# A transformer layer's first stage in another order: input and one weight pair loaded first, first projection ahead of three of four combination passes

## The chip, the cores and the metric

The kernel runs on one core of a Trainium2 chip. Its time is the device time of one execution in microseconds (us), the median of several runs. Five engines work side by side: TensorE (PE) multiplies matrices into the accumulator memory PSUM (`ps`, eight banks), ScalarE (ACT), VectorE (DVE) and GpSimd (POOL) work on elements, and SyncE (SP) issues transfers (DMA) from the chip's memory. Each engine runs its own list of instructions strictly in order, and waits on semaphores that others raise.

## What is computed

The reference normalises the input `x` (8 sequences of 100 tokens, width 512), puts it through a decoder layer, and then through a layer of experts whose two gates share one pair of weights. Cut to the part that the change touches:

```
x = _layernorm(x)                              # per token
q = tgt @ in_proj_w[:D].T + in_proj_b[:D]      # query projection
k = tgt @ in_proj_w[D:2 * D].T + in_proj_b[D:2 * D]
v = tgt @ in_proj_w[2 * D:].T + in_proj_b[2 * D:]
attn = softmax(q k^T / sqrt(D))
sa = (attn v) @ out_proj_w.T + out_proj_b
```

Behind it follow cross attention on 722 context rows of each sequence, a feed-forward layer of width 2048, three normalisations and the experts.

## The kernel before

The 800 tokens are worked on in two halves of 400 (`h` = 0 and 1), as features by tokens: a matrix of width 512 is four chunks of 128 rows (`KC` = 4). Every fp32 product is made from two reduced-precision parts: a value is split into a high part (ScalarE writes `..H`) and the rest (`..L`, by VectorE or GpSimd), and TensorE adds high by high, low by high and high by low. So each product of 128 by 128 by 400 is three matmuls, and weights must be split before they are used.

The value and the output weights are combined ahead into one matrix (`U_VO`) by four passes over `k`, each of `combine_high(k)` (four matmuls VH by OH) and `combine_low(k)` (four VL by OH, four VH by OL), in the banks 4 to 7. TensorE first runs `WARM_UP` = 11 small matmuls (seen as 22 in the profile) on the identity matrix.

The input goes through another chain: the loads `load_x` and `load_x_tail` bring the tokens to `tok` (96 rows and the last 4 of each sequence apart), `statistics` on VectorE makes mean and variance, `inverse_deviation` on GpSimd raises the variance to the power of -1/2 (`rstd`), `normalise` scales two of a half's four sequences on VectorE and two on ScalarE, `to_features` transposes them on TensorE (sixteen transposes into banks 0 to 3), and `norm_features` splits the result into `XH` and `XL`. Then `unit(U_Q, 0)` projects the queries of half 0 (48 matmuls into banks 0 to 3) and `unit(U_K, 0)` the keys. A group of `unit` waits until the bank it writes was read.

The raw weights come in `VR` and `OR` (value and output, a chunk each per `load_vo`), `WR` (query, in two transfers of two chunks) and `WRK` (key). The order of all this is written out by hand, for each engine in its own list; SyncE's list sets the order of the transfers, which all go through one queue to the same DMA engines. All that stands behind this first stage (the second halves, self attention and so on) is not touched.

Of the kernel before, what the change touches and what calls it, by code (L numbers as in the profile page):

```python
# [12 lines left out]
P = 128  # L13
# [159 lines left out]
def build(nc, x, ctxt, ctxn, wvo, wts, consts, g3, be3, out):  # L173
    with ExitStack() as ctx:
# [69 lines left out]
        VH, VL = [sb(name, "R4", o, [P, KC, D], F32R) for name, o in (("VH", 0), ("VL", 8192))]  # L244
        OH, OL = [sb(name, "R1", o, [P, KC, D], F32R) for name, o in (("OH", 0), ("OL", 8192))]
        VR, OR = [sb(name, "R2", o, [P, KC, D]) for name, o in (("VR", 0), ("OR", 8192))]
# [40 lines left out]

        x_loaded = [sem("x_loaded%d" % i) for i in range(4)]
        x_tail = [sem("x_tail0"), sem("x_tail1")]
# [209 lines left out]
        def _(sp):  # L499
            def load_x(i):  # L500
                sp.dma_start(tok[0:TA, 2 * i:2 * i + 2, :], x[2 * i:2 * i + 2, 0:TA].rearrange("b t d -> t b d")
                             ).then_inc(x_loaded[i], 16)

# [9 lines left out]

            load_vo(0)
            load_vo(1)
            load_x_tail(0)
            load_x(0)
            load_x(1)
            load_vo(2)
            load_vo(3)  # L520
            sp.dma_start(WR[:, 0:2, :], wts[0, :, 0:2, :]).then_inc(w0_loaded, 16)
            sp.dma_start(WR[:, 2:KC, :], wts[0, :, 2:KC, :]).then_inc(weights_loaded, 16)
            load_x_tail(1)
            load_x(2)
            load_x(3)
            sp.dma_start(cst[:, :], consts).then_inc(consts_loaded, 16)
# [98 lines left out]
        def _(pool):  # L625
# [73 lines left out]

            split_o(1)  # L700
            inverse_deviation(0, 0)
            pool.wait_ge(nmr_ready, 1)
            split_o(3)
            split_weights(U_Q, range(KC // 2))
            for k in range(KC // 2, KC):
                pool.wait_ge(w_high, KC * WHOLE.index(U_K) + k + 1)
                pool.tensor_tensor(WL[SLOT[U_K]][:, k, :], WRK[:, k, :], raw(WH[SLOT[U_K]][:, k, :]),
                                   ALU.subtract).then_inc(wk_low_pool, 1)
            inverse_deviation(1, 1)
            pool.wait_ge(vo_made, KC)  # L710
# [44 lines left out]
        def _(pe):  # L755
# [182 lines left out]
            def combine_low(k):  # L938

                pe.wait_ge(v_low, k + 1)  # L940
                for e in range(KC):
                    pe.matmul(ps[:, 4 + e, :], VL[:, k, e * P:(e + 1) * P], OH[:, k, :], start=False, stop=False)
                if k % 2 == 0:
                    pe.wait_ge(o_low, k // 2 + 1)
                else:
                    pe.wait_ge(o_low_pool, k // 2 + 1)
                for e in range(KC):
                    mm = pe.matmul(ps[:, 4 + e, :], VH[:, k, e * P:(e + 1) * P], OL[:, k, :], start=False,
                                   stop=(k == KC - 1))
                    if k == KC - 1:  # L950
                        mm.then_inc(vo_made, 1)
# [156 lines left out]
            for _ in range(WARM_UP):  # L1108
                pe.matmul(ps[:, 3, 0:P], ident[:, :], ident[:, :], start=True, stop=True)
            for k in range(KC - 1):  # L1110
                combine_high(k)
                combine_low(k)
            combine_high(KC - 1)
            to_features(0, 0, tiles[0])
            combine_low(KC - 1)
            unit(U_Q, 0)
            unit(U_K, 0, [0])
            to_features(0, 1, tiles[1])
            unit(U_K, 0, [1, 2, 3])
            unit(U_Q, 1)  # L1120
# [85 lines left out]
        def _(act):  # L1206
# [211 lines left out]

            for k in range(KC):
                split_vo(k)  # L1420
            normalise(0, 0, tiles[0])
            split_weights(U_Q, 0)
            split_weights(U_Q, 1)
            norm_features(0, 0)
            split_weights(U_Q, 2)
            split_weights(U_Q, 3)
            for e in range(KC):
                act.wait_ge(vo_made, e + 1)
                act.activation(WH[SLOT[U_VO]][:, e, :], ps[:, 4 + e, :], ACT.Copy).then_inc(vo_high, 1)
            act.wait_ge(consts_loaded, 16)  # L1430
            act.activation(wgS[:, :, 0:NE], cst[:, C_WG:C_ALL].rearrange("p (k e) -> p k e", k=KC),
                           ACT.Copy).then_inc(small_high, 1)
            for k in range(KC):
                split_weights(U_K, k)
            unit(U_Q, 0, [0, 1, 2])
            normalise(0, 1, tiles[1])
            unit(U_Q, 0, [3])
            unit(U_K, 0, [0])
            norm_features(0, 1)
            unit(U_K, 0, [1, 2, 3])  # L1440
            split_ct(0, 0)
# [112 lines left out]
        def _(dve):  # L1554
# [166 lines left out]
            def statistics(h, before, js=range(HB)):  # L1721

                for j in js:
                    b = HB * h + j
                    if before is None:
                        if j % 2 == 0:
                            dve.wait_ge(x_loaded[b // 2], 16)
                        if j == 0:
                            dve.wait_ge(x_tail[h], 16)
                        st = dve.bn_stats(bnst[:, b, :], tok[:, b, :])  # L1730
                    else:
                        dve.wait_ge(to_tok, before + j + 1)
                        st = dve.bn_stats(bnst[:, b, :], ps[0:T, 4 + j, :])
                if js[-1] < HB - 1:
                    return
                settle(st)
                for j in range(HB):
                    ag = dve.bn_aggr(mv[:, HB * h + j, :], bnst[:, HB * h + j, :])
                settle(ag)
                dve.tensor_scalar(veps[:, :], mv[:, HB * h:HB * (h + 1), 1], EPS, None,  # L1740
                                  ALU.add).then_inc(stats_ready, 1)
# [169 lines left out]
            def split_o(k):  # L1911
                dve.wait_ge(o_high, k + 1)
                dve.tensor_tensor(OL[:, k, :], OR[:, k, :], raw(OH[:, k, :]), ALU.subtract).then_inc(o_low, 1)

            split_v(0)
            split_o(0)
            split_v(1)
            statistics(0, None)
            split_v(2)
            split_o(2)  # L1920
            normalise(0, 0, tiles[0])
            split_v(3)
            norm_features(0, 0)
            for k in range(KC // 2, KC):
                dve.wait_ge(w_high, k + 1)
                dve.tensor_tensor(WL[SLOT[U_Q]][:, k, :], WR[:, k, :], raw(WH[SLOT[U_Q]][:, k, :]),
                                  ALU.subtract).then_inc(w0_low, 1)
            for e in range(KC):
                dve.wait_ge(vo_high, e + 1)
                dve.tensor_tensor(WL[SLOT[U_VO]][:, e, :], ps[:, 4 + e, :], raw(WH[SLOT[U_VO]][:, e, :]),  # L1930
                                  ALU.subtract).then_inc(vo_low, 1)
            statistics(1, None)
            split_weights(U_K, 0)
            split_weights(U_K, 1)
            normalise(0, 1, tiles[1])
            norm_features(0, 1)
# [190 lines left out]
```

## Time and profile before

| | |
|---|---|
| median of 3 runs | 513.67 us (513.58 to 514.22) |
| profiled execution | 513.71 us, its span 511.9 us |
| mean granted clock of TensorE | 0.998 of full |
| busy: TensorE matmul | 504.6 us, 99% of the span |
| busy: VectorE, ScalarE, GpSimd | 375.7, 243.0, 140.0 us |
| transfers | 53.76 MB, mean 105 GB/s |

The span goes from the first to the last instruction; what the profiled execution's own time has beyond it lies around the program. Times of single instructions are counted from the start of the span. Matmuls are pipelined, so the busy times of two neighbours overlap; their pace is read from their starts.

### The profile page before, as it was taken

Reading aid. Unit: us, or ns where it says so; the run is one execution under the profiler, and the core shown is the slowest. Engines: PE = TensorE matmul, PEld = TensorE weight load, DVE = VectorE, ACT = ScalarE, POOL = GpSimd, SP = SyncE. Lnnn points to the kernel's source line nnn. Section 1 sums busy time; section 2 is a strip of 40 time slices with the busy share of each in tenths; the row PEclk is TensorE's granted clock in tenths of the full one; section 3 lists DMA queues with packets and bytes.
Section 4 is the critical chain, followed back from the end, with each engine's and each line's share of the span. In section 5 each row is a group of like instructions: output and inputs, shape, how many; then the busy total and the mean of one; then the engine's idle time right before and its main releaser. Section 6 shows DMA issues by size and latency. Waiting matters only on the chain.

```text
span 511.9 us, 7634 instructions
## 1 busy us (share of the span) xinstructions
PE 504.6 (99%) x2958; PEld 484.8 (95%) x2958; DVE 375.7 (73%) x643; ACT 243.0 (47%) x429; POOL 140.0 (27%) x105
## 2 busy tenths in 40 slices
PE   8999999999999999999999999999999999999997
PEld 6899999889988888999999999999999899999996
DVE  3853769796799996787699776368586878786645
ACT  3853652465598886164654334206536532442210
POOL 2530541014013134254504000445438403030000
PEclk9999999999999999999999999999999999999999
DMA  8951222031589962204521242002202022202004
GB/s 224 345 206 59 60 82 83 1 116 56 216 262 341 307 227 67 82 13 125 124 80 77 88 159 83 1 1 80 85 2 67 17 83 76 89 0 83 2 0 129
DMA packets 18444, 53.76 MB, mean 105 GB/s; under 512 B 1640, under 2 KB 2440, under 8 KB 15848
## 3 DMA queue, kind: packets, MB, share of 16 engines
q1 hardware_dynamic: 18348, 53.20, 31.7%
q8 instruction: 24, 0.39, 0.3%
q10 hardware_dynamic: 60, 0.07, 0.1%
q14 instruction: 12, 0.10, 0.1%
HBM read 51.63 MB, written 1.64 MB: 104 GB/s over the span
## 4 chain that ended last, share of the span: by engine, by line
PE 91%; DVE 3%; DMA 3%; ACT 1%; SPq 0%; POOL 0%; issue 0%; DVEq 0%; ACTq 0%
PE ps L799 18%; PE ps L801 18%; PE ps L800 18%; PE ps L863 5%; PE ps L862 5%; PE ps L861 5%; PE ps L917 3%; PE ps L891 2%; PE ps L1059 2%; PE ps L1060 2%; PE ps L1061 2%; DMA tok<-x_in 2%; PE ps L1033 2%; PE ps L1035 2%; PE ps L1034 2%; PE ps L1005 1%
## 5 line engine op out<-in xcount | busy, mean ns | idle before, releaser
L799 PE MATMUL ps<-AH,WH 128*128 128x400 f32 x284 | 98.6, 347 | 0.3 <-DVE AL L1592 0.3
L801 PE MATMUL ps<-AH,WL 128*128 128x400 f32 x284 | 98.0, 345 | 0.0
L800 PE MATMUL ps<-AL,WH 128*128 128x400 f32 x284 | 97.9, 345 | 0.0
L799 PE MATMUL ps<-XH,WH 128*128 128x400 f32 x192 | 66.9, 348 | 0.1
L801 PE MATMUL ps<-XH,WL 128*128 128x400 f32 x192 | 66.3, 345 | 0.0
L800 PE MATMUL ps<-XL,WH 128*128 128x400 f32 x192 | 66.2, 345 | 0.0
L642 POOL TENSOR_TENSOR WL<-WR,WH 128x512 fp32r<-128x512 f32 x30 | 42.9, 1460 | 69.0 <-ACT WH L1226 69.0
L799 PEld LDWEIGHTS ps<-AH,WH 128*128 128x128 f32 x284 | 53.4, 188 | 0.8 <-DVE AL L1592 0.6
L800 PEld LDWEIGHTS ps<-AL,WH 128*128 128x128 f32 x284 | 53.4, 188 | 0.0
L801 PEld LDWEIGHTS ps<-AH,WL 128*128 128x128 f32 x284 | 53.4, 188 | 0.0
L1226 ACT ACTIVATE WH<-WR 128x512 fp32r<-128x512 f32 x60 | 34.0, 624 | 24.3 <-DMA WR<-wts_in 24.3
L1305 ACT ACTIVATE AH<-AT 128x400 fp32r<-128x400 f32 x40 | 21.2, 538 | 49.5 <-DVE AT L1652 32.6
L1614 DVE TENSOR_TENSOR acc<-ps,acc 128x400 f32<-128x400 f32 x47 | 26.6, 569 | 17.9 <-PE ps L801 17.7
L1571 DVE TENSOR_TENSOR ctL<-ctR,ctH 128x1444 fp32r<-128x1444 f32 x16 | 28.6, 1795 | 12.6 <-ACT ctH L1234 12.5
L799 PEld LDWEIGHTS ps<-XH,WH 128*128 128x128 f32 x192 | 36.1, 188 | 0.8 <-issue 0.3
L800 PEld LDWEIGHTS ps<-XL,WH 128*128 128x128 f32 x192 | 36.1, 188 | 0.0
L801 PEld LDWEIGHTS ps<-XH,WL 128*128 128x128 f32 x192 | 36.1, 188 | 0.0
L647 POOL TENSOR_TENSOR cnL<-cnR,cnH 128x1024 fp32r<-128x1024 f32 x7 | 17.1, 2438 | 53.6 <-ACT cnH L1240 53.6
L1657 DVE SCALAR_TENSOR_TENSOR AL<-AT,AH 128x400 fp32r<-128x400 f32 x40 | 28.1, 722 | 1.6
L1256 ACT ACTIVATE AT<-ps,cst 128x400 f32<-128x400 f32 x16 | 9.5, 595 | 40.9 <-PE ps L801 40.9
L636 POOL TENSOR_TENSOR rstd<-veps,nhalf 100x4 f32<-100x4 f32 x10 | 14.0, 1395 | 51.9 <-DVE veps L1740 51.7
L1240 ACT ACTIVATE cnH<-cnR 128x1024 fp32r<-128x1024 f32 x24 | 24.9, 1057 | 1.6 <-DMA cnR<-ctxn_in 1.6
(244 smaller groups left out, 1188.8 us busy)
## 6 DMA issues: line engine op xcount, KB each, us to landing
WR<-wts_in SPq DMA_DIRECT2D x19, 1024.0 KB, 4.8
ctR<-ctxt_in SPq DMA_DIRECT2D x16, 722.0 KB, 5.9
cnR<-ctxn_in SPq DMA_DIRECT2D x16, 512.0 KB, 5.1
cnR<-ctxn_in SPq DMA_DIRECT2D x8, 256.0 KB
tok<-x_in SPq DMA_DIRECT2D x4, 384.0 KB, 9.8
tok<-x_in SPq DMA_DIRECT2D x1, 1536.0 KB
cnR<-ctxn_in SPq DMA_DIRECT2D x8, 160.0 KB
VR<-wvo_in SPq DMA_DIRECT2D x4, 256.0 KB, 6.9
```

Of the source, the lines that this page charges most:

```text
L642: pool.tensor_tensor(WL[SLOT[n]][:, k, :], WR[:, k, :], raw(WH[SLOT[n]][:, k, :]), ALU.subtract).then_inc(w_low_pool, 1)
L799: pe.matmul(dst, wh, half(mh, h, k), start=(k == 0), stop=False)
L800: pe.matmul(dst, wh, half(ml, h, k), start=False, stop=False)
L801: mm = pe.matmul(dst, wl, half(mh, h, k), start=False, stop=(k == KC - 1))
L861: pe.matmul(dst, ah[:, k, cols], bh[:, k, :], start=(k == 0), stop=False)
L862: pe.matmul(dst, ah[:, k, cols], bl[:, k, :], start=False, stop=False)
L863: mm = pe.matmul(dst, al[:, k, cols], bh[:, k, :], start=False, stop=(k == 1))
L1226: act.activation(WH[SLOT[n]][:, k, :], raw_weights[:, k, :], ACT.Copy).then_inc(w_high, 1)
L1240: act.activation(cnH[:, 2 * i:2 * i + 2, :], raw_cn(b, i), ACT.Copy).then_inc(cn_high, 1)
L1571: dve.tensor_tensor(ctL[b % 2][:, 2 * i:2 * i + 2, 0:M], raw_ct(b, i), raw(ctH[b % 2][:, 2 * i:2 * i + 2, 0:M]), ALU.subtract).then_inc(ct ...
L1614: dve.tensor_tensor(half(acc, h, e), src, half(acc, h, e), ALU.add).then_inc(dve_evac, 1)
L1657: dve.scalar_tensor_tensor(out=half(AL, h, e), in0=half(AT, h, e), scalar=0.0, in1=raw(half(AH, h, e)), op0=ALU.max, op1=ALU.subtract).the ...
```

## The change

The transfers are issued in another order: the first half's input is in front, now in four transfers of one sequence each where it was two of two, then chunk 0 of V and O, then both transfers of the query weight, and then the rest. Each sequence of the input has a semaphore of its own. TensorE does `combine_high(0)`, the transposes, `combine_low(0)`, then the whole query projection of half 0 (chunks 0 and 1 of all four groups, then chunks 2 and 3), and then the passes 1 to 3; the key projection has one more group ahead of the second transposes. The lists of ScalarE, VectorE and GpSimd are ordered after it. `OH` and `OL` move by one half's size within their region, away from `qT`, which is now written while they are still read.

```diff
-        OH, OL = [sb(name, "R1", o, [P, KC, D], F32R) for name, o in (("OH", 0), ("OL", 8192))]
+        OH, OL = [sb(name, "R1", HS + o, [P, KC, D], F32R) for name, o in (("OH", 0), ("OL", 8192))]
...
-            def load_x(i):
-                sp.dma_start(tok[0:TA, 2 * i:2 * i + 2, :], x[2 * i:2 * i + 2, 0:TA].rearrange("b t d -> t b d")
-                             ).then_inc(x_loaded[i], 16)
+            def load_x(h):
+                for b in range(HB * h, HB * (h + 1)):
+                    sp.dma_start(tok[0:TA, b, :], x[b, 0:TA]).then_inc(x_loaded[b], 16)
...
-            load_vo(0)
-            load_vo(1)
             load_x_tail(0)
             load_x(0)
+            load_vo(0)
+            sp.dma_start(WR[:, 0:2, :], wts[0, :, 0:2, :]).then_inc(w0_loaded, 16)
+            sp.dma_start(WR[:, 2:KC, :], wts[0, :, 2:KC, :]).then_inc(weights_loaded, 16)
+            load_vo(1)
+            load_x_tail(1)
             load_x(1)
             load_vo(2)
             load_vo(3)
-            sp.dma_start(WR[:, 0:2, :], wts[0, :, 0:2, :]).then_inc(w0_loaded, 16)
-            sp.dma_start(WR[:, 2:KC, :], wts[0, :, 2:KC, :]).then_inc(weights_loaded, 16)
-            load_x_tail(1)
-            load_x(2)
-            load_x(3)
...
-            split_o(1)
             inverse_deviation(0, 0)
-            pool.wait_ge(nmr_ready, 1)
-            split_o(3)
+            split_o(0)
             split_weights(U_Q, range(KC // 2))
+            split_o(2)
+            inverse_deviation(1, 1)
...
-            for k in range(KC - 1):
+            combine_high(0)
+            to_features(0, 0, tiles[0])
+            combine_low(0)
+            for chunks in ([0, 1], [2, 3]):
+                for e in range(KC):
+                    pe.wait_ge(x_ready, e + 1)
+                    unit(U_Q, 0, [e], chunks)
+            for k in range(1, KC):
                 combine_high(k)
                 combine_low(k)
-            combine_high(KC - 1)
-            to_features(0, 0, tiles[0])
-            combine_low(KC - 1)
-            unit(U_Q, 0)
-            unit(U_K, 0, [0])
+            unit(U_K, 0, [0, 1])
             to_features(0, 1, tiles[1])
-            unit(U_K, 0, [1, 2, 3])
+            unit(U_K, 0, [2, 3])
...
-            for k in range(KC):
-                split_vo(k)
-            normalise(0, 0, tiles[0])
+            split_vo(0)
             split_weights(U_Q, 0)
             split_weights(U_Q, 1)
+            normalise(0, 0, tiles[0])
             norm_features(0, 0)
             split_weights(U_Q, 2)
             split_weights(U_Q, 3)
+            for k in range(1, KC):
+                split_vo(k)
...
-            split_v(0)
-            split_o(0)
-            split_v(1)
-            statistics(0, None)
-            split_v(2)
-            split_o(2)
-            normalise(0, 0, tiles[0])
-            split_v(3)
+            statistics(0, None)
+            normalise(0, 0, tiles[0])
+            split_v(0)
             norm_features(0, 0)
```

TensorE's list from its start, before (each row is a run of like instructions; OH, VH and so on are the split weights, `ident,tok` the transposes, XH with WH the query projection):

```order
L1109 MATMUL ps<-ident 128x128 x11
L936 MATMUL ps<-OH,VH 128x512 x4
L942 MATMUL ps<-OH,VL 128x512 x4
L948 MATMUL ps<-OL,VH 128x512 x4
...
L936 MATMUL ps<-OH,VH 128x512 x4
L891 MATMUL ps<-ident,tok 128x100 x16
L942 MATMUL ps<-OH,VL 128x512 x4
L948 MATMUL ps<-OL,VH 128x512 x4
L799 MATMUL ps<-XH_49,WH_104 128x400
```

And in the change, at the same place:

```order
L1106 MATMUL ps<-ident 128x128 x11
L933 MATMUL ps<-OH,VH 128x512 x4
L888 MATMUL ps<-ident,tok 128x100 x16
L939 MATMUL ps<-OH,VL 128x512 x4
L945 MATMUL ps<-OL,VH 128x512 x4
L796 MATMUL ps<-XH_49,WH_104 128x400
...
L933 MATMUL ps<-OH,VH 128x512 x4
L939 MATMUL ps<-OH,VL 128x512 x4
L945 MATMUL ps<-OL,VH 128x512 x4
L796 MATMUL ps<-XH_49,WH_105 128x400
```

Ten groups of four stood ahead of the transposes, now one does; nine stand behind the query projection. ScalarE's list at its start (VH and OH are the splits of V and O, WH_104 those of the query weight, `tok` the normalisation), as a difference:

```order
 L1415 ACTIVATE VH<-VR 128x512
 L1417 ACTIVATE OH<-OR 128x512
-L1415 ACTIVATE VH<-VR 128x512
-L1417 ACTIVATE OH<-OR 128x512
-L1415 ACTIVATE VH<-VR 128x512
-L1417 ACTIVATE OH<-OR 128x512
-L1415 ACTIVATE VH<-VR 128x512
-L1417 ACTIVATE OH<-OR 128x512
+L1226 ACTIVATE WH_104<-WR 128x512 x2
 L1329 ACTIVATE tok<-tok,nmr,rstd 100x512 x2
-L1226 ACTIVATE WH_104<-WR 128x512 x2
 L1338 ACTIVATE XH_49<-ps 128x400 x4
```

Two splits of the query weight now stand ahead of the normalisation, and three pairs of V and O splits behind it. SyncE's list at its start in the change:

```order
L507 DMA tok<-x_in 4x4x512
L502 DMA tok<-x_in 96x512 x4
L511 DMA VR<-wvo_in 128x512
L512 DMA OR<-wvo_in 128x512
L517 DMA WR<-wts_in 128x1024
L518 DMA WR<-wts_in 128x1024
```

Before, the chunks 0 and 1 of V and O (four transfers of 256 KB) stood ahead of the tail and the first half's input, and the query weight behind all of V and O. Now the input is first, one pair of V and O chunks follows, and then the query weight.

## Rows read from the trace of the kernel before

**Rows 1.** The page: busy time and share of the span by engine.
```profile
PE 504.6 (99%) x2958; PEld 484.8 (95%) x2958; DVE 375.7 (73%) x643; ACT 243.0 (47%) x429; POOL 140.0 (27%) x105
```

**Rows 2.** All waits of TensorE from 20.94 us on.
```profile
PE ps L799 <- DVE AL L1592: 0.3, 1, 0.3
PE ps L917 <- DVE acc L2075: 0.2, 1, 0.2
```

**Rows 3.** Timeline of TensorE (PE): start us, us, line, operands, count, idle before.
```profile
5.92 1.20 PE L936 MATMUL ps<-OH,VH 128*128 128x512 f32 x4
13.42 1.19 PE L936 MATMUL ps<-OH,VH 128*128 128x512 f32 x4 [1.18 <-ACT OH L1417]
16.27 1.07 PE L936 MATMUL ps<-OH,VH 128*128 128x512 f32 x4
17.64 1.59 PE L891 MATMUL ps<-ident,tok 100*128 100x100 f32 x16 [0.29 <-DVE tok L1752]
19.01 1.17 PE L942 MATMUL ps<-OH,VL 128*128 128x512 f32 x4
20.94 0.35 PE L799 MATMUL ps<-XH,WH 128*128 128x400 f32 x1
21.13 0.34 PE L800 MATMUL ps<-XL,WH 128*128 128x400 f32 x1
```

**Rows 4.** Chain of work that ended last, 0 to 21 us: start, us, what.
```profile
0.74 0.38 SPq L511
...
3.37 8.11 DMA tok<-x_in
...
13.49 2.01 POOL rstd L636
...
15.68 1.91 DVE tok L1752 x2
```

**Rows 5.** Timeline of VectorE (DVE).
```profile
10.14 2.65 DVE L1730 BATCH_NORM_STATS2 bnst<-tok 100x6 f32<-100x512 f32 x4 [1.43 <-DMA tok<-x_in]
18.77 2.02 DVE L1768 TENSOR_TENSOR XL<-ps,XH 128x400 fp32r<-128x400 f32 x4 [0.59 <-ACT XH L1338]
```

**Rows 6.** Timeline of ScalarE (ACT).
```profile
4.06 0.63 ACT L1415 ACTIVATE VH<-VR 128x512 fp32r<-128x512 f32 x1 [2.04 <-DMA VR<-wvo_in]
7.34 0.63 ACT L1415 ACTIVATE VH<-VR 128x512 fp32r<-128x512 f32 x1 [1.48 <-DMA VR<-wvo_in]
8.50 0.63 ACT L1417 ACTIVATE OH<-OR 128x512 fp32r<-128x512 f32 x1 [0.53 <-DMA OR<-wvo_in]
15.72 1.52 ACT L1329 ACTIVATE tok<-tok,nmr,rstd 100x512 f32<-100x512 f32 x2 [1.00 <-DVE nmr L1747]
17.14 1.14 ACT L1226 ACTIVATE WH<-WR 128x512 fp32r<-128x512 f32 x2
23.43 2.19 ACT L1226 ACTIVATE WH<-WRK 128x512 fp32r<-128x512 f32 x4 [0.40 <-DMA WRK<-wts_in]
```

**Rows 7.** Timeline of SyncE's queue, which issues the transfers.
```profile
3.00 0.82 SPq L501 DMA_DIRECT2D tok<-x_in  x2
6.42 0.61 SPq L521 DMA_DIRECT2D WR<-wts_in  x1
```

**Rows 8.** Transfers issued from 6.4 to 7 us: KB, us from issue to landing.
```profile
WR<-wts_in SPq DMA_DIRECT2D x1, 512.0 KB, 9.0
```

**Rows 9.** Timeline of GpSimd (POOL).
```profile
17.84 2.75 POOL L642 TENSOR_TENSOR WL<-WR,WH 128x512 fp32r<-128x512 f32 x2 [0.54 <-ACT WH L1226]
```

**Rows 10.** Warm-up matmuls of two stretches: ns min/median/max, first and last start.
```profile
L1109 PE MATMUL ps<-ident x8: 421/421/580, 1.7 to 3.4; 128*128 128x128 f32 x8
...
L1109 PE MATMUL ps<-ident x5: 274/275/421, 4.7 to 5.3; 128*128 128x128 f32 x5
```

**Rows 11.** Stretches behind the last matmul; 1.00 and 0.50 are the granted clock.
```profile
508.75:510.25 1.50, 0.00 (x0) 0.00 (x0) 0.54 (x3) 0.00 (x0) 0.00 (x0) 1.00 0.62 188
510.25:510.75 0.50, 0.00 (x0) 0.00 (x0) 0.00 (x0) 0.00 (x0) 0.00 (x0) 0.50 0.68 196
```

More of the change, by code:

```diff
@@ L285, in build @@
         ps = ctx.enter_context(nc.psum_tensor("ps", [P, 8, 512], F32))
-        x_loaded = [sem("x_loaded%d" % i) for i in range(4)]
+        x_loaded = [sem("x_loaded%d" % b) for b in range(B)]
         x_tail = [sem("x_tail0"), sem("x_tail1")]
@@ L708, in _ @@
                                    ALU.subtract).then_inc(wk_low_pool, 1)
-            inverse_deviation(1, 1)
             pool.wait_ge(vo_made, KC)
@@ L942, in combine_low @@
                     pe.matmul(ps[:, 4 + e, :], VL[:, k, e * P:(e + 1) * P], OH[:, k, :], start=False, stop=False)
-                if k % 2 == 0:
+                if k % 2:
                     pe.wait_ge(o_low, k // 2 + 1)
@@ L1426, in _ @@
             split_weights(U_Q, 3)
+            for k in range(1, KC):
+                split_vo(k)
+            act.wait_ge(consts_loaded, 16)
+            act.activation(wgS[:, :, 0:NE], cst[:, C_WG:C_ALL].rearrange("p (k e) -> p k e", k=KC),
+                           ACT.Copy).then_inc(small_high, 1)
+            unit(U_Q, 0, [0, 1])
+            normalise(0, 1, tiles[1])
+            unit(U_Q, 0, [2, 3])
+            for k in range(KC):
+                split_weights(U_K, k)
             for e in range(KC):
@@ L1429, in _ @@
                 act.activation(WH[SLOT[U_VO]][:, e, :], ps[:, 4 + e, :], ACT.Copy).then_inc(vo_high, 1)
[L1430 to L1438, printed above, removed]
+            unit(U_K, 0, [0, 1])
             norm_features(0, 1)
-            unit(U_K, 0, [1, 2, 3])
+            unit(U_K, 0, [2, 3])
             split_ct(0, 0)
@@ L1725, in statistics @@
                     if before is None:
-                        if j % 2 == 0:
-                            dve.wait_ge(x_loaded[b // 2], 16)
+                        dve.wait_ge(x_loaded[b], 16)
                         if j == 0:
@@ L1927, in _ @@
                                   ALU.subtract).then_inc(w0_low, 1)
+            split_v(1)
+            split_o(1)
+            statistics(1, None)
+            split_v(2)
+            normalise(0, 1, tiles[1])
+            split_v(3)
+            split_o(3)
+            split_weights(U_K, 0)
+            split_weights(U_K, 1)
             for e in range(KC):
@@ L1931, in _ @@
                                   ALU.subtract).then_inc(vo_low, 1)
[L1932 to L1935, printed above, removed]
             norm_features(0, 1)
```

## Prediction

> **What bounds the kernel now.** I read the page first: TensorE's matmuls are busy in 99% of the span [rows 1]. Busy alone proves little, so I read next who TensorE waits for. From 20.94 us, where the first projection starts, to the end there are only two waits, of 0.3 and 0.2 us [rows 2]. So nothing behind 20.94 us can absorb a delay, and nothing there can be won: an edit of the first stage is worth what it moves the moment at which TensorE gets into its unbroken run.
>
> Then the order of events ahead of that run. TensorE warms up from 1.7 us [rows 10], starts the first combination pass at 5.92, and the four passes (three groups of four matmuls each) and sixteen transposes fill 15.02 us up to 20.94 [rows 3]. A pass without a wait takes 13.42 to 16.27 = 2.85 us [rows 3]. Twelve groups are 4 x 2.85 = 11.4, the transposes 17.64 to 19.01 = 1.37, so idle is 15.02 - 12.8 = 2.2 us. That is all that any order could win here without starting earlier than 5.92. The chain of waits names what limits the transposes: the transfer of the input, that lands at 11.48 [rows 4], statistics until 12.79 [rows 5], the power on POOL to 15.50, the normalisation to 17.59 [rows 4]. The passes cover this chain: they need only V and O, which land first.
>
> **The change, part by part.** It adds and removes no arithmetic. TensorE now does only the first group of pass 0 ahead of the transposes, where it had ten; nine groups (3 x 2.85 = 8.55 us) move behind the first projection. In the changed order the common point is reached 8.55 us later after the transposes than before. With the transposes at time S, the run is late by S + 8.55 - 17.64, thus S has to be 9.1 us for no change. The whole question is S.
>
> *When the input lands.* Landings against the KB issued up to them, counting every transfer on the queue: 256 KB at 4.0, 768 KB at 7.3, 1024 KB at 8.5 (the ends of ScalarE's waits for DMA [rows 6]), 1440 KB (32 for the tail, 384 of input) at 10.1 [rows 5], 1824 KB at 11.48 [rows 4], and the first half of the query weight, 3360 KB, at 6.42 + 9.0 = 15.4 [rows 7, 8]. Now tail and input are 800 KB in front: some 7.5 us. From below, an issue takes 0.41 us [rows 7] and the fastest transfer was there 3.3 us after its issue (0.74 [rows 4] to 4.06 [rows 6]), so the last of the four input transfers, issued near 2.4, lands no earlier than 5.7. V and O of pass 0 come to 1312 KB, 9.6 between the points above; the weight pair's first half to 1824 KB, exactly the sum that landed at 11.48: I take 11.5. Its bounds: from 7.5 at the fast pace of (3360 - 1824) / (15.4 - 11.5) = 394 KB per us, 10.1; and with the 9.0 us that the same transfer took from its issue, now near 3.75, 12.75.
>
> *The chain by VectorE.* Last input 7.5, its statistics 2.65/4 = 0.66 [rows 5], then as before from the end of statistics to the transposes 17.64 - 12.79 = 4.85 us [rows 3, 5]: 13.0.
>
> *The chain by ScalarE.* Two of the four token blocks are normalised by ScalarE, and its queue now has the two splits of the query weight ahead of that (they stood behind it). The splits take 1.14 us and the normalisation 1.52 [rows 6]. Behind the waiting split stands everything that the transposes need: 11.5 + 1.14 + 1.52 = 14.2. This is later than 13.0, so S = 14.2, and the wait of the weight transfer takes the place of the wait for the input. TensorE meanwhile has one group of about 1 us, at 10.3 (O lands at 9.6, 0.63 for the split [rows 6]), and idles for the rest of 6.0 to 14.2. First term: 14.2 + 8.55 - 17.64 = **+5.1 us**.
>
> *Does a wait follow?* Behind the transposes the high and low halves of the features take from 17.64 to 20.79 in the trace [rows 3, 5], 3.15 us; TensorE has 1.37 + 1.93 (19.01 to 20.94 [rows 3]) of work for it, and gets to the first projection at 17.5. The low half of the first two weight chunks, 2.75 us on POOL [rows 9], starts after POOL's power (over at 10.9) and one O split of half that length, at 12.3, and is over by 15.1. Chunks 2 and 3 are split on ScalarE behind the features (4 x 0.5) by 17.7 and on VectorE by 19.0; the projection now goes through chunks 0 and 1 of all four groups first, 24 matmuls of 0.18 = 4.4 us [rows 3], to 21.9. The passes 1 to 3 then begin at 26.3, far behind their splits. The key weight landed at 23.4 [rows 6] with the same bytes ahead of it, and is wanted at about 35. The second transposes want all the low halves of the combined matrix, and have 4.4 us of projection between, in which ScalarE and VectorE have to split a matrix of four chunks (0.63 us a chunk on ScalarE [rows 6], VectorE one chunk behind it: 3.2 us at most). I cost all of that at nothing; the tightest is the features' low half, 17.35 against 17.5, and there each group waits only for its own chunk; the others have 1 us or more.
>
> *The clock.* The warm-up shows both levels: its matmuls take 421 ns until about 4.9 us, 275 ns from there [rows 10], which is TensorE at 1.2 and then at 2.4 GHz, after 3.2 us of work. The end shows the fall: idle from 508.75, granted clock 1.00 up to 510.25, then 0.50 [rows 11]. Before, work follows the warm-up at once and the clock stays up. Now TensorE idles from 6.0 to about 10.3, longer than the time it took to fall at the end, so I expect transposes and the first passes at 1.2 GHz from 14.2 until again 3.2 us of work are over. Half of that is lost: **+1.6 us**. The bounds are 0 (it stays up, or the one group at 10.3 brings it back in time) and 3.2 (it takes twice as long).
> The Trainium skill (TensorE: Matmul & The Clock Gate, Part 1) says the same of idle stretches and a return to half rate, and in Part 4 that the full clock does not engage for transposes. The trace does not bear that out for transposes behind dense passes: the sixteen (two instructions each) at 17.64 take 1.37 us, 43 ns an instruction of 100 columns, which is 2.4 GHz. For transposes behind an idle stretch it has no row, and there the rule would give rival 2: they stay at half rate themselves and the clock rises only behind them.
>
> **Sum.** 5.1 + 1.6 = +6.7 us on the profiled execution's 513.71 (its span of 511.9 and 1.8 around it), which agrees with the median of 513.67: **520.4 us**, 1.3% slower.
>
> **Rivals.**
> 1. *The clock doesn't fall.* For it: one group of work stands inside the gap, and no row shows whether that keeps the clock up. Against it: 4.3 us of idle beforehand. 513.7 + 5.1 = 518.8.
> 2. *Transposes don't bring the clock back.* They take 1.37 us more at half rate [rows 3], before the 3.2 us begin: 1.4 more, 521.8. Nothing in the rows contradicts it.
> 3. *The weight pair lands early* (10.1, the fast pace), so VectorE's chain decides: S = 13.0, +3.9 and the clock's 1.6: 519.2, without the fall 517.6. Against: the queue's landings before 11.5 go at about 200 KB per us from 4.0 (1568 KB in 7.5 us). The other way, at 12.75, S = 15.4, +6.3 + 1.6: 521.6.
> 4. *Not slower.* The input's chain is so short that TensorE reaches the transposes by 9.1. It decides there: last input in by 9.1 - 4.85 - 0.66 = 3.6 us, when the first 256 KB of all landed at 4.0 before, and with the weight splits not in the way. With the input at the 5.7 bound, S is 11.2 and the kernel still +2.1 (515.8). The idle 2.2 us before 20.94 can't help, as none of it is removed. For it speaks only that each input block now has its own transfer and its statistics begin at about 4: a gain of 2 us in VectorE, none after the last block. If it did hold, the time would be 513 to 514.
>
> **How the numbers follow.** Forecast 520.4: 0.47. Rival 1: 0.17. Rival 2: 0.13. Rival 3: 0.12 early and 0.05 late. Rival 4: 0.03 for a time like before's or below; 0.03 for something unforeseen, half of it faster. The bounds of the sum are +3.9 (517.6) with no fall, and +6.3 + 3.2 (523.2). The low end goes a little under the former for an input landing ahead of 7.5; the high end stays under the latter, which needs both at once: 517.0 to 522.6. About 0.2% (1 us) is what a measurement of this kernel can tell from no change. Slower 0.94, the same 0.03, faster 0.03.
>
> **What would show it.** In the changed profile: the first transposes at about 14, waiting for ScalarE's normalised tokens, and ScalarE waiting for the weight pair's DMA until 11.5; TensorE idle for some 7 us between 6 and 14; granted clock 0.50 somewhere from 8 to 17, with 512-column matmuls at twice their spacing of 2.85/12 = 0.24 us; and then no waits of more than 0.3 us until the tail. The third key-projection group and the self scores should stand 6 to 7 us later than before. I am wrong if the input lands by 4 us, if TensorE's unbroken run begins earlier than before, or if a wait elsewhere in the run shows up, most likely at the second transposes or at the key weight's splits.

## The result and the profile after

The changed kernel takes 519.33 us (518.63 to 520.60, 5 runs), the kernel before 513.67 us (513.10 to 514.22, 5 runs): a ratio of 1.011, 95% interval 1.0099 to 1.0121. It is 5.7 us slower, inside the range of 517.0 to 522.6 and 1.1 us under the forecast of 520.4. The profiled execution took 520.60 us, 6.9 more than the profiled one of before.

The page of the changed kernel, its lines of the span, of busy time and of the granted clock in 40 slices:

```profile
span 518.8 us, 7637 instructions
PE 507.8 (98%) x2958; PEld 487.8 (94%) x2958; DVE 374.8 (72%) x643; ACT 243.3 (47%) x429; POOL 138.5 (27%) x105
...
PEclk8799999999999999999999999999999999999999
```

TensorE's busy time rose by 3.2 us against [rows 1], though it does the same matmuls: a part of them ran at the lower clock, which the first two slices show (8 and 7 tenths).

TensorE's timeline (start us, us, line, operands, count, idle before), to be read against [rows 3]:

```profile
9.92 2.07 PE L933 MATMUL ps<-OH,VH 128*128 128x512 f32 x4 [3.93 <-ACT OH L1417]
13.14 2.93 PE L888 MATMUL ps<-ident,tok 100*128 100x100 f32 x16 [1.15 <-ACT tok L1329]
15.77 2.05 PE L939 MATMUL ps<-OH,VL 128*128 128x512 f32 x4
17.62 1.56 PE L945 MATMUL ps<-OL,VH 128*128 128x512 f32 x4
19.01 0.34 PE L796 MATMUL ps<-XH,WH 128*128 128x400 f32 x1
...
27.75 1.09 PE L933 MATMUL ps<-OH,VH 128*128 128x512 f32 x4
40.33 1.54 PE L888 MATMUL ps<-ident,tok 100*128 100x100 f32 x16
```

Between the warm-up and the first combination group it idles 3.9 us, then 1.2 us between that group and the transposes, which start at 13.14. The transposes take 13.14 to 15.77 = 2.63 us, where they took 1.37, and pass 0's two low groups 15.77 to 19.01 = 3.24 us where two groups took 1.93. From the projection on it runs at its pace of before, with nine groups between 27.75 us and the key projection. All its waits in the whole run:

```profile
PE ps L933 <- ACT OH L1417: 3.9, 1, 3.9
PE ps L1106 <- POOL ones L630: 1.7, 1, 1.7
PE ps L888 <- ACT tok L1329: 1.2, 1, 1.2
PE ps L1056 <- DVE ptL L1818: 0.3, 1, 0.3
PE ps L796 <- DVE AL L1593: 0.3, 1, 0.3
PE ps L914 <- DVE acc L2075: 0.2, 1, 0.2
```

The last two stand in the kernel before as well [rows 2]. ScalarE's timeline says what the transposes waited for, in place of [rows 6]:

```profile
9.23 0.63 ACT L1417 ACTIVATE OH<-OR 128x512 fp32r<-128x512 f32 x1 [0.45 <-DMA OR<-wvo_in]
10.52 1.15 ACT L1226 ACTIVATE WH<-WR 128x512 fp32r<-128x512 f32 x2 [0.66 <-DMA WR<-wts_in]
11.58 1.51 ACT L1329 ACTIVATE tok<-tok,nmr,rstd 100x512 f32<-100x512 f32 x2
```

The two splits of the query weight wait for its transfer until 10.52, and the normalisation stands behind them until 13.09. VectorE and GpSimd had their parts long before (in place of [rows 5], and of the power in [rows 4]):

```profile
5.78 1.29 DVE L1730 BATCH_NORM_STATS2 bnst<-tok 100x6 f32<-100x512 f32 x2 [0.54 <-DMA tok<-x_in]
8.91 1.00 DVE L1752 TENSOR_SCALAR tok<-tok,mv,rstd 100x512 f32<-100x512 f32 x2
```

```profile
7.77 1.02 POOL L634 TENSOR_TENSOR rstd<-veps,nhalf 100x4 f32<-100x4 f32 x1 [5.64 <-DVE veps L1740]
```

The last input lands before 6.4 us, the power takes 1.02 us instead of 2.01, and VectorE's share of the tokens is ready at 9.91.

The clock, by stretches of the start (busy us and count of PE, PEld, DVE, ACT and POOL, then the granted clock, the share of the DMA engines and GB/s), as in [rows 11]:

```profile
8.00:9.00 1.00, 0.00 (x0) 0.00 (x0) 0.17 (x2) 0.63 (x1) 0.80 (x1) 0.69 1.07 295
9.00:10.00 1.00, 0.08 (x1) 0.09 (x1) 1.00 (x3) 0.63 (x1) 0.06 (x1) 0.50 1.02 344
...
18.00:19.00 1.00, 1.00 (x4) 0.78 (x3) 1.00 (x3) 0.75 (x3) 0.00 (x0) 0.69 1.06 383
19.00:20.00 1.00, 1.00 (x7) 0.98 (x6) 1.00 (x3) 0.96 (x2) 0.00 (x0) 1.00 1.13 419
```

It fell to one half (1.2 GHz) at 8.4 us, in the idle stretch, and was back at 2.4 GHz from 18.6.

The rest of the loss can be read off two late landmarks: one of cross attention's groups of transposes, and the last matmuls. Before, they stood at:

```profile
158.63 0.68 PE L1046 MATMUL ps<-ident,prob 100*128 100x100 f32 x6
...
508.31 0.42 PE L917 MATMUL ps<-ident,acc 128*100 128x128 f32 x2 [0.24 <-DVE acc L2075]
```

After the change:

```profile
164.86 0.68 PE L1043 MATMUL ps<-ident,prob 100*128 100x100 f32 x6
170.18 0.47 PE L1056 MATMUL ps<-cnH,ptH 128*100 128x512 f32 x1 [0.30 <-DVE ptL L1818]
...
515.18 0.42 PE L914 MATMUL ps<-ident,acc 128*100 128x128 f32 x2 [0.24 <-DVE acc L2075]
```

The delay is 164.86 - 158.63 = 6.2 us at the first landmark, and 515.18 - 508.31 = 6.9 us at the end. The 0.6 us between are lost just behind the first landmark, at the wait of 0.3 us at 170.18 and the groups after it. The chain of the changed kernel's profile goes through a context transfer there (start, us, what):

```profile
159.78 7.24 DMA cnR<-ctxn_in
```

This part is not the change's. The stretch between the two landmarks takes 349.7 us in the profiled execution of before, 350.3 in this one, and 349.2 in a second execution of the same changed kernel; over all profiled executions it lies between 349.2 and 351.2. The chain of before goes through a context transfer too, later on (171.52, for 6.98 us). What the change does to the time is read from the first landmark.

### The profile page after: what moved, and what is told of

Its sections match the earlier page's. It is cut to its first block, busy times and chain, and to the rows that moved or that the text cites. A ratio compares the mean times of both kernels' runs of the same rounds, so it can differ in the third digit from the quotient of the medians.

```text
span 518.8 us, 7637 instructions
## 1 busy us (share of the span) xinstructions
PE 507.8 (98%) x2958; PEld 487.8 (94%) x2958; DVE 374.8 (72%) x643; ACT 243.3 (47%) x429; POOL 138.5 (27%) x105
## 3 DMA queue, kind: packets, MB, share of 16 engines
HBM read 51.63 MB, written 1.64 MB: 103 GB/s over the span
## 4 chain that ended last, share of the span: by engine, by line
PE 92%; DMA 3%; DVE 2%; ACT 1%; SPq 1%; issue 0%; DVEq 0%; ACTq 0%
PE ps L796 18%; PE ps L798 18%; PE ps L797 18%; PE ps L860 5%; PE ps L859 5%; PE ps L858 5%; PE ps L914 3%; PE ps L888 2%; PE ps L1056 2%; PE ps L1058 2%; PE ps L1057 2%; PE ps L1030 2%; PE ps L1032 2%; PE ps L1031 2%; DMA cnR<-ctxn_in 1%; PE ps L1002 1%
## 5 line engine op out<-in xcount | busy, mean ns | idle before, releaser
L1615 DVE TENSOR_TENSOR acc<-ps,acc 128x400 f32<-128x400 f32 x47 | 26.7, 570 | 18.3 <-PE ps L798 18.1
L1572 DVE TENSOR_TENSOR ctL<-ctR,ctH 128x1444 fp32r<-128x1444 f32 x16 | 28.7, 1807 | 10.6 <-ACT ctH L1234 10.5
L634 POOL TENSOR_TENSOR rstd<-veps,nhalf 100x4 f32<-100x4 f32 x10 | 12.4, 1237 | 55.9 <-DVE veps L1740 55.8
```

The source lines that it names most:

```text
L1572: dve.tensor_tensor(ctL[b % 2][:, 2 * i:2 * i + 2, 0:M], raw_ct(b, i), raw(ctH[b % 2][:, 2 * i:2 * i + 2, 0:M]), ALU.subtract).then_inc(ct ...
L1615: dve.tensor_tensor(half(acc, h, e), src, half(acc, h, e), ALU.add).then_inc(dve_evac, 1)
```

## Experiments

All of them are edits of the changed kernel except the two that say otherwise. "S" is the start of the transposes, as in the prediction. Each ratio is to the kernel before in the same rounds (medians 513.6 to 513.8 us), with its 95% interval.

**A longer warm-up.**

```diff
-WARM_UP = 11
+WARM_UP = 30
```

> The changed kernel with 30 warm-up matmuls instead of 11: 19 more at 0.21 us each fill TensorE from 5.9 to about 9.9 us, where the first combination group begins. Theory (a late start plus a fallen clock): granted clock stays 1.00 through the transposes, these still start at 13.1, because the extra matmuls move nothing else; the time is before's plus 13.1 + 8.55 - 17.64 = 4.0 us, 517.7. Rival (the delay is all in the late start, or the clock falls in the remaining gap of 1.2 us anyway): 519.3, as without them. Second rival (the extra matmuls delay the first group and the transposes): above 519.3.

Measured: 517.18 us (516.56 to 518.26), ratio to before 1.0068 (1.0050 to 1.0086), mean clock 0.999. TensorE's timeline in its profile:

```profile
10.30 1.19 PE L933 MATMUL ps<-OH,VH 128*128 128x512 f32 x4
12.81 1.59 PE L888 MATMUL ps<-ident,tok 100*128 100x100 f32 x16 [1.32 <-ACT tok L1329]
```

The first group and the transposes are where they were, within 0.4 us, the granted clock is 1.00 up to the last matmuls, and the time is 2.2 us less than the changed kernel's: the fallen clock is a cost of its own.

**The normalisation ahead of the splits on ScalarE.**

```diff
             split_vo(0)
+            normalise(0, 0, tiles[0])
             split_weights(U_Q, 0)
             split_weights(U_Q, 1)
-            normalise(0, 0, tiles[0])
```

> The changed kernel with ScalarE's normalisation ahead of its two splits of the query weight. Theory (the splits' wait for the weight transfer until 10.5 holds the transposes): the normalisation starts when the split of O is over at 9.86, is done by 11.4, so the transposes start at 11.4 instead of 13.1 and all that follows is 1.7 us earlier: about 517.6 to 518. Rival (the transposes wait for something else too: VectorE's share or the low half of the weights): the time stays at 519.3, and a new wait of 1.7 us shows on TensorE at the first projection.

Measured: 518.23 us (517.90 to 519.87), ratio 1.0084 (1.0067 to 1.0101). The profiled execution was the slowest of the four, and shows no gain: its transposes start at 13.10, as its own chain of the input was late. VectorE's timeline:

```profile
7.80 0.69 DVE L1730 BATCH_NORM_STATS2 bnst<-tok 100x6 f32<-100x512 f32 x1 [1.64 <-DMA tok<-x_in]
10.25 1.24 DVE L1747 SCALAR_TENSOR_TENSOR nmr<-mv,rstd 100x4 f32<-100x4 f32 x1 [1.14 <-POOL rstd L634]
```

The last sequence landed at 7.8 here, and one small instruction (`nmr`) took 1.24 us where it took 0.16 in the changed kernel; what stood beside it on GpSimd is told below, at VectorE's chain. The median is 1.1 us less, but its interval touches the changed kernel's. By itself this run does not settle it; the pair further down does.

**Both edits.**

> Both edits: 30 warm-up matmuls and the normalisation first. Theory: the two costs add, transposes at 11.4 and the clock stays up: before's plus 11.4 + 8.55 - 17.64 = 2.3 us, 516.0. What is left is the moved passes alone. Rival (another cost of the new order that neither edit touches, such as a wait at the second transposes): 517 or more.

Measured: 516.42 us (515.75 to 518.91), ratio 1.0060 (1.0041 to 1.0080). TensorE's timeline:

```profile
11.42 1.59 PE L888 MATMUL ps<-ident,tok 100*128 100x100 f32 x16 [0.26 <-DVE tok L1752]
36.06 1.54 PE L888 MATMUL ps<-ident,tok 100*128 100x100 f32 x16
```

Transposes at 11.42 and the clock at 1.00. From S to the second transposes are 36.06 - 11.42 = 24.64 us; in the changed kernel it was 40.33 - 13.14 = 27.19, so the clock cost 2.55 us there. What is left, 515.75 - 513.71 = 2.0 us in the profiled times, is the price of the moved passes less what the earlier start gives back.

**The new lists on the old order of transfers.**

```diff
+            load_vo(0)
+            load_vo(1)
             load_x_tail(0)
             load_x(0)
-            load_vo(0)
-            sp.dma_start(WR[:, 0:2, :], wts[0, :, 0:2, :]).then_inc(w0_loaded, 16)
-            sp.dma_start(WR[:, 2:KC, :], wts[0, :, 2:KC, :]).then_inc(weights_loaded, 16)
-            load_vo(1)
-            load_x_tail(1)
-            load_x(1)
             load_vo(2)
             load_vo(3)
+            sp.dma_start(WR[:, 0:2, :], wts[0, :, 0:2, :]).then_inc(w0_loaded, 16)
+            sp.dma_start(WR[:, 2:KC, :], wts[0, :, 2:KC, :]).then_inc(weights_loaded, 16)
+            load_x_tail(1)
+            load_x(1)
```

> The changed kernel's engine lists with the transfers in the order of before (V and O of passes 0 and 1 first, the query weight behind all of V and O). Theory (what costs is TensorE's order, and the new order of transfers softens it): the weight lands at 15.4, its splits and ScalarE's normalisation follow, transposes at 18.1, so before's plus 18.1 + 8.55 - 17.64 = 9.0 us and 1.6 to 2.9 of clock: 524 to 526. Rival (the loss comes from loading V and O later, TensorE's order is neutral): about 514.

Measured: 525.00 us (524.67 to 525.16), ratio 1.0217 (1.0202 to 1.0232). ScalarE's timeline, then TensorE's:

```profile
16.84 1.15 ACT L1226 ACTIVATE WH<-WR 128x512 fp32r<-128x512 f32 x2 [10.28 <-DMA WR<-wts_in]
```

```profile
19.45 2.93 PE L888 MATMUL ps<-ident,tok 100*128 100x100 f32 x16 [11.65 <-ACT tok L1329]
```

ScalarE waits 10.3 us for the weight, and TensorE 11.7 us for ScalarE. The weight landed at 16.8 us, not at 15.4, so S was 19.45 and not 18.1. That the wait for the query weight is what holds the transposes is plainest here.

**The old lists on the new order of transfers** (the kernel before, `x_loaded` by sequence).

```diff
-            load_vo(0)
-            load_vo(1)
             load_x_tail(0)
             load_x(0)
-            load_x(1)
+            load_vo(0)
+            sp.dma_start(WR[:, 0:2, :], wts[0, :, 0:2, :]).then_inc(w0_loaded, 16)
+            sp.dma_start(WR[:, 2:KC, :], wts[0, :, 2:KC, :]).then_inc(weights_loaded, 16)
+            load_vo(1)
+            load_x_tail(1)
+            load_x(1)
             load_vo(2)
             load_vo(3)
...
```

> The kernel before, all engine lists as before, with the change's order of transfers alone (each input sequence with its own transfer and semaphore). Theory (this half of the change delays V and O, on which TensorE's ten groups ahead of the transposes depend): the first group at about 9.9 us instead of 5.9, and the last pass waits for its V and O, which in the changed kernel were split at 21.6; with 1 + 1.4 + 1.9 us of work behind that, the projection begins near 25.8 instead of 20.9. So +4.9 us and up to 2.6 for the clock: 518.5 to 521. Rival (the new order of transfers is harmless and only the engine lists cost): about 514. Together with the run of the new lists on the old transfers (525.0) it says how the two halves combine: the changed kernel (519.3) should not be worse than either half alone.

Measured: 519.06 us (518.13 to 521.12), ratio 1.0107 (1.0085 to 1.0129). TensorE's timeline:

```profile
9.28 1.84 PE L934 MATMUL ps<-OH,VH 128*128 128x512 f32 x4 [2.72 <-ACT OH L1415]
15.09 1.21 PE L934 MATMUL ps<-OH,VH 128*128 128x512 f32 x4 [1.21 <-ACT OH L1415]
19.54 1.20 PE L934 MATMUL ps<-OH,VH 128*128 128x512 f32 x4 [1.40 <-ACT OH L1415]
23.30 1.54 PE L889 MATMUL ps<-ident,tok 100*128 100x100 f32 x16
```

The passes wait for V and O (2.7, 1.2 and 1.4 us), and the transposes come at 23.30 with only two groups behind them. Each half alone loses: 11.4 us for the lists, 5.3 for the transfers, 5.7 to 6.2 for both together. So the new transfers take away about half of what the new lists cost. The new lists take nothing off the cost of the new transfers: the medians of both together (519.33 and 519.87) are not below that of the transfers alone (519.06), and the intervals overlap.

**The gap before the transposes filled.**

```diff
             combine_high(0)
+            for _ in range(3):
+                pe.matmul(ps[:, 3, 0:P], ident[:, :], ident[:, :], start=True, stop=True)
             to_features(0, 0, tiles[0])
```

> The changed kernel with three more identity matmuls (about 1.1 us at the lower clock) in the idle time between its first combination group and the transposes. Theory (the clock returns late, at 18.6 us, because the work from 9.9 on is broken by an idle stretch of 1.2 us): it returns some us earlier and the time is 1 to 2 us less than the changed kernel's in the same rounds, the transposes starting at 13.1 as before. Rival (that gap has no part in it; only the 3.9 us before the first group or the transposes matter): no difference to the changed kernel.

> The changed kernel again, on the same chip and in the same rounds as the others of this call, so that they can be compared with it. Both theories: 519.3, between 518.6 and 520.6 as before.

Measured: 519.09 us (517.88 to 520.84), and the changed kernel beside it 519.87 us (518.94 to 523.08); ratios 1.0107 (1.0085 to 1.0129) and 1.0129 (1.0103 to 1.0155). The medians don't tell them apart. Their two profiled executions differ in the stretch behind S. With the gap filled, TensorE's timeline and the clock in two stretches:

```profile
11.23 1.48 PE L1109 MATMUL ps<-ident 128*128 128x128 f32 x6
13.70 1.59 PE L888 MATMUL ps<-ident,tok 100*128 100x100 f32 x16 [0.99 <-DVE tok L1754]
38.35 1.54 PE L888 MATMUL ps<-ident,tok 100*128 100x100 f32 x16
```

```profile
12.00:13.00 1.00, 0.71 (x4) 0.42 (x2) 1.00 (x2) 0.53 (x1) 1.00 (x1) 0.71 1.05 232
13.00:16.00 3.00, 2.30 (x20) 2.16 (x21) 2.40 (x5) 1.70 (x5) 0.36 (x1) 1.00 1.07 240
```

The changed kernel in the same rounds, TensorE's timeline:

```profile
13.72 2.93 PE L888 MATMUL ps<-ident,tok 100*128 100x100 f32 x16 [2.13 <-ACT tok L1329]
41.31 1.54 PE L888 MATMUL ps<-ident,tok 100*128 100x100 f32 x16
```

From S to the second transposes are 24.65 us with the gap filled, 27.59 without; the profiled times are 517.88 and 520.46. In the first the clock is back at 12.6, in the second at 20.1. But of the six executions with the filled gap three had a mean clock of 0.989 or 0.990 and 519.9 to 520.8 us, and of the changed kernel's six one had 0.999. So an early return happens with the gap filled and, it seems, without; that the filled gap brings it about is not shown. The two values of S, 13.70 and 13.72, agree by chance: with the gap filled the transposes waited for VectorE, in the changed kernel for ScalarE.

**Only the input by sequence** (the kernel before, `load_x` and `statistics` as in the change, the order of transfers as before).

```diff
-            def load_x(i):
-                sp.dma_start(tok[0:TA, 2 * i:2 * i + 2, :], x[2 * i:2 * i + 2, 0:TA].rearrange("b t d -> t b d")
-                             ).then_inc(x_loaded[i], 16)
+            def load_x(h):
+                for b in range(HB * h, HB * (h + 1)):
+                    sp.dma_start(tok[0:TA, b, :], x[b, 0:TA]).then_inc(x_loaded[b], 16)
...
-                        if j % 2 == 0:
-                            dve.wait_ge(x_loaded[b // 2], 16)
+                        dve.wait_ge(x_loaded[b], 16)
```

> The kernel before with only one detail of the change: one transfer and one semaphore for each input sequence instead of one for two. Theory (small gain): the last statistics follow the last landing by 0.7 us instead of 1.3, so the transposes come 0.3 us earlier, where TensorE waits 0.29 us for them: 513.3, which a measurement can hardly tell from 513.6. Rival (the smaller transfers land later and eat it up): 513.6 to 514.

Measured: 513.61 us (512.04 to 515.40, 12 runs), ratio 0.9990 (0.9977 to 1.0004). The gain of 0.3 us was expected, and the measurement can't tell it from none. In the profiled execution the first landmark stands at 158.27, 0.36 us earlier than before, and the last matmuls at 508.70, 0.39 later.

**What ScalarE's order costs at full clock.** The kernel with the longer warm-up and the one with both edits again, in the same rounds.

> The changed kernel with 30 warm-up matmuls again, with more rounds and beside the next kernel, to settle what ScalarE's order costs when the clock is out of the question. Both theories: 517.2, transposes at about 12.8.

> 30 warm-up matmuls and the normalisation ahead of the weight's splits again, in the same rounds. Theory (ScalarE's split waits for the weight transfer, and the transposes behind it): transposes 1.4 us earlier than in the run beside it, and the time 1.4 us less, about 515.8. Rival (it only looked so in one profiled execution; landings vary as much): the difference of the medians is under 0.5 us.

Measured: 517.58 us (516.86 to 520.87, 6 runs) with the splits ahead, 516.11 us (515.30 to 518.50, 7 runs) with the normalisation ahead, 1.5 us less; ratios 1.0080 (1.0054 to 1.0107) and 1.0046 (1.0028 to 1.0065). The transposes with the splits ahead, in TensorE's timeline:

```profile
13.08 1.59 PE L888 MATMUL ps<-ident,tok 100*128 100x100 f32 x16 [1.52 <-ACT tok L1329]
```

With the normalisation ahead, ScalarE's and TensorE's timelines:

```profile
9.46 1.51 ACT L1329 ACTIVATE tok<-tok,nmr,rstd 100x512 f32<-100x512 f32 x2
```

```profile
11.08 1.54 PE L888 MATMUL ps<-ident,tok 100*128 100x100 f32 x16
```

S moves from 13.08 to 11.08, 2.0 us, and the profiled times from 517.23 to 515.30, 1.9 us. The intervals of the ratios overlap a little, but six of the seven executions lie below all six of the other kernel. Not all of the 2.0 us is ScalarE's order: VectorE's share was ready at 11.68 in the first and at 10.07 in the second. With VectorE as late as in the first, S would have come to about 11.7, 1.4 us earlier, which is the theory's number and near the medians' 1.5.

**The transposes first of all.** As the last kernel, and:

```diff
-            combine_high(0)
             to_features(0, 0, tiles[0])
+            combine_high(0)
             combine_low(0)
...
-            split_vo(0)
             normalise(0, 0, tiles[0])
+            split_vo(0)
             split_weights(U_Q, 0)
```

> As the run before, and in addition the transposes ahead of the first combination group, with the normalisation ahead of the splits of V and O on ScalarE: the input's chain now waits for nothing but itself. Theory (what is left is the moved passes): transposes at 10 to 10.5, but ten groups of 0.91 us stand behind them instead of nine, so before's plus 10.3 + 9.1 - 17.64 = 1.8 us: 515.5, near the run beside it, and still slower than before. Rival (with the input's chain free of all others this order beats before): under 513.

Measured: 516.86 us (515.85 to 517.91), ratio 1.0051 (1.0034 to 1.0068). TensorE's transposes, and its longest wait behind the warm-up:

```profile
10.91 1.59 PE L888 MATMUL ps<-ident,tok 100*128 100x100 f32 x16 [0.69 <-ACT tok L1329]
```

```profile
PE ps L1056 <- DVE ptL L1818: 1.0, 2, 0.7
```

Nothing but the input's own chain is ahead of the transposes now, and they still start at 10.91; ten groups stand behind them. The sum gives 10.91 + 9.1 - 17.64 = +2.4; at the first landmark the delay is 161.32 - 158.63 = 2.7, and the other 1.5 us of the 4.2 that this execution lost come in cross attention, 1.0 of them as waits. The 0.3 us between 2.4 and 2.7 are open. No version of this order came under the kernel before.

## Why the forecast held, step by step

**One sum explains the executions.** A pass behind the query projection takes 8.2/3 = 2.73 us, as 27.75 to 35.94 hold nine groups of 0.91. With S from the profile and the clock up, the kernel should stand S + 8.2 - 17.64 behind the kernel before. Where the clock had fallen, the stretch from S to the second transposes is longer than the 24.65 us that it takes at full clock, and this excess is added. The delay is read at the first landmark, in front of the uneven part of cross attention (all in us):

| profiled execution | S | S + 8.2 - 17.64 | clock | sum | delay read |
|---|---|---|---|---|---|
| changed kernel | 13.14 | 3.70 | 2.55 | 6.25 | 6.23 |
| changed kernel, second | 13.72 | 4.28 | 2.94 | 7.22 | 7.15 |
| longer warm-up | 12.81 | 3.37 | 0 | 3.37 | 3.34 |
| longer warm-up, again | 13.08 | 3.64 | 0 | 3.64 | 3.60 |
| normalisation first | 13.10 | 3.66 | 3.03 | 6.69 | 6.66 |
| both edits | 11.42 | 1.98 | 0 | 1.98 | 1.93 |
| both edits, again | 11.08 | 1.64 | 0 | 1.64 | 1.55 |
| old transfers | 19.45 | 10.01 | 1.58 | 11.59 | 11.56 |
| gap filled | 13.70 | 4.26 | 0 | 4.26 | 4.25 |

The kernel with the transposes first is off by 0.3, all others are within 0.1 us. By the last matmuls up to 0.6 us more has come or gone (1.5 with the transposes first), in cross attention. That is the prediction's frame, and it holds for the first stage: an edit is worth S, plus what is moved behind it, plus the clock.

**S.** The mechanism was right: ScalarE's splits wait for the weight pair, and the transposes wait behind them. The size was off: 13.1 for 14.2, and 13.7 in the second execution. The weight landed at 10.5 and at 11.1, not 11.5, between the two bounds; with the longer warm-up and with the gap filled, which leave the transfers as they are, at 10.2, 10.5 and 10.0. So the same 1824 KB landed at times that differ by 1.1 us, and all of them before 11.5. The new mix has the weight's larger rows in it, which may be why; that was not tried. The pair at full clock shows the mechanism: two splits' place on ScalarE is worth some 1.5 us.

**VectorE's chain.** The forecast had it at 13.0; in the two executions of the changed kernel it was ready at 9.9 and 11.2, ahead of ScalarE's 13.1 and 13.7. The error cost nothing there. It would have misled in the rival that the weight lands early, whose 519.2 rests on it: with the weight in time, S would have come to 11.1 to 11.4, as the two profiles with both edits show.

The 4.85 us from the statistics to the transposes were no fixed price, and the reason can be read from the traces: VectorE and GpSimd hold each other up. Before, GpSimd's power took 2.00 us (13.49 to 15.49) with two of VectorE's splits beside it (13.32 to 14.61); in all executions of the new lists it took 1.02 to 1.03 in the first half, with VectorE idle. The other way round, the change drops `pool.wait_ge(nmr_ready, 1)`, behind which GpSimd let VectorE's small instruction go first, and puts its split of O right behind the power. GpSimd's and VectorE's timelines with the gap filled:

```profile
9.45 1.27 POOL L651 TENSOR_TENSOR OL<-OR,OH 128x512 fp32r<-128x512 f32 x1
```

```profile
9.51 1.23 DVE L1749 SCALAR_TENSOR_TENSOR nmr<-mv,rstd 100x4 f32<-100x4 f32 x1 [1.14 <-POOL rstd L634]
10.67 2.98 DVE L1754 TENSOR_SCALAR tok<-tok,mv,rstd 100x512 f32<-100x512 f32 x2
```

GpSimd's split starts 0.06 us ahead of `nmr`, which then ends 0.02 us behind it and takes 1.23 us instead of 0.16; the two blocks behind it, beside two more of GpSimd's splits, take 2.98 instead of 1.00. VectorE was ready at 13.65 there, ScalarE at 12.53, so in this execution VectorE set S. The same start of 0.06 or 0.07 us later, and 1.22 to 1.24 us for `nmr`, stand in three more (longer warm-up, normalisation first, old transfers). In the changed kernel's first execution the split of O came at 9.94, after VectorE was done. No run put the wait back.

**The moved groups.** 8.2 us instead of 8.55. The pass from which I took 2.85 us began behind a wait, and its first group of four took 1.03 us (13.42 to 14.45) where later ones take 0.91.

**The clock.** It fell as forecast, and it cost 2.55 us in the first profiled execution and 2.94 in the second (27.59 - 24.65), not 1.6. The step that failed in size is the taking over of 3.2 us from the warm-up as the work that goes by until the clock is back: here it was 18.6 - 13.1 = 5.5 us of unbroken work, and 6.3 in the second. Half of it was lost, as forecast. With the old transfers it was 3.4 us (19.45 to 22.8), and the cost 1.6. The rival that the clock stays up (518.8) fell with its profile; the longer warm-up shows what it would have given, 517.2. The rival that transposes do not bring it back (521.8) is not settled: with the old transfers the clock rose at 22.8, 0.8 us after the transposes' end, too early for it; in the second profile of the changed kernel it rose 3.7 us after their end, as it would have it. The Trainium skill's line (TensorE: Matmul & The Clock Gate, Part 4) that the full clock does not engage for transposes is not borne out where it is up already: with the gap filled, the sixteen at 13.70 take 1.37 us at clock 1.00, against 2.63 at 0.50 in the changed kernel. These two times show it better than the prediction's 43 ns for each of two instructions; the profile lists one matmul for each transpose, 86 ns apart.

**No wait behind.** Right for the first stage: no wait of TensorE between 13.1 us and cross attention, and the delay of 6.2 us, inside the 6 to 7 of the prediction's signs, is unchanged at the first landmark. Behind it the profiled execution lost 0.6 us more than the kernel before, and the second lost 0.5 less. The prediction costed nothing in that stage. Two executions of one kernel differ by 1.1 us there, so the change is not shown to cause any of it.

**The sum.** In the profiled execution: 13.14 + 8.2 - 17.64 = 3.7, the clock 2.55, cross attention 0.6, together 6.9, which is what was measured. The forecast's 6.7 had 5.1 and 1.6: one error of 1.4 too much and one of 1.0 too little, which cancel. That the total came so near is luck; each term was off by more than a third. The median of 5.7 us more is under this. The other four executions had mean clocks of 0.990 to 0.992 instead of 0.988; they have no profile, so their share of clock and of cross attention is open.

**The side of the rivals.** "Not slower" needed the transposes at 9.1; with the measured pass it is 9.4. Freed of everything else they start at 10.9. Before, TensorE had 2.2 us of idle ahead of its run, by the prediction's sum; the new order has 3.9 + 1.2 = 5.1 us of it, because the work that filled the wait for the input was put behind it.

## What to carry to other kernels

When one engine is busy from some point to the end, look for the work that needs the least input and keep it in front of the chain that is longest: here V and O need one transfer and one split, the input a transfer, statistics, a power and a normalisation. Each instruction that is moved from in front of a late start to behind it costs its full time. And look in every engine's list for an instruction that waits for a transfer ahead of one that the bounding engine needs. An idle stretch of the bounding engine can cost more than its own length through the clock, and cheap filler work (here 19 extra small matmuls) gives that part back. Last, a wait that seems to serve nothing may keep one engine's long instruction from starting just ahead of another's short one: ask that of VectorE and GpSimd before it is dropped.

## What the runs showed of the hardware

- The granted clock stayed at one half for 10.2 us in each of four executions: 8.4 to 18.6 and 9.9 to 20.1 (the changed kernel), 9.4 to 19.6 (normalisation first), 12.6 to 22.8 (old transfers). In the first three a group of matmuls and then an idle stretch of 1.2 to 2.1 us came ahead of the unbroken work; in the last, TensorE did nothing from 7.8 to 19.45. Where work without a break had begun about when the clock fell, it was back after 3.4 us (9.2 to 12.6 with the gap filled, 9.6 to 13.0 with the old lists). In the kernel before, after its idle start, it was back after 3.2 us of work. The Trainium skill (TensorE: Matmul & The Clock Gate, Part 1) says that sustained work releases the clock; these runs agree, but the unbroken work that went by until the clock was back differed from 3.2 to 6.5 us.
- The power on GpSimd took 1.02 to 1.03 us alone for 100 by 4 elements, 1.38 or 1.39 with VectorE's splits beside its first 0.5 to 1.1 us, and 2.00 with them beside its first 1.1 us in the kernel before. VectorE's normalisation took 0.54 us a block alone and 1.5 to 1.6 a block when a split of GpSimd had started ahead of it. That the overlap decides it is read from the traces; no run isolates it.
- One combination group of 512 columns takes 1.03 to 1.05 us as the first behind a wait, and 0.91 in a run without one.
